# A GRU over 256 steps: the order of loads and of the first products before step 1

## The chip, the core and the metric

The kernel runs on one core of one Trainium2 chip. The metric is the device time of one execution in microseconds (us). The kernel before took 1025.57 us (median of three runs, 1025.18 to 1025.68).

## What is computed

With 16 sequences of 256 steps and 512 channels:

```
x = x + causal_depthwise_conv(x, cond)        # 16 taps per channel, the taps are cond [16, 512]
h = cond                                      # initial state, [16, 512]
for t in range(256):                          # GRU cell, W_ih and W_hh are [512, 1536]
    gi = x[:, t] @ W_ih + b_ih
    gh = h @ W_hh + b_hh
    r = sigmoid(i_r + h_r); z = sigmoid(i_z + h_z)
    n = tanh(i_n + r * h_n)
    h = (1 - z) * n + z * h
    out[:, t] = x[:, t] + h
```

Everything is float32.

## The kernel before, in words

The 512 channels are laid out as four chunks `c` of 128 partitions. The 1536 gate columns are split into two halves `f`, which run a little apart so that one half's gate arithmetic lies beside the other half's matmuls. A **group** is four matmuls of 32 output partitions (j = 0 to 3), which run beside each other in the array, and each of which the trace keeps as two records; so eight records of L328 or L318 are one group.

*Products* (`product(q)`, L318) are x @ W_ih. One q is one group: two steps (index m), a half f and a chunk c. They are done ahead of use: a pair of steps has 8 groups, and 4 groups stand beside every step. *Recurrences* (`recur(t, f, c)`, L328) are h @ W_hh, 8 groups a step. Both add into the PSUM tile `pg[m % 3][f]`, into which ScalarE has copied the biases (`seed`, L437). Within a PSUM tile the h_n part has its own columns (0 to 64), r and z follow, and i_n is last. For a recurrence to write n, r and z as one matmul, ScalarE copies W_hh's n columns in front of its r and z columns (L455). Only for the last chunk of step 0 this copy isn't waited for: `recur_first` makes two matmuls of each (L339 r and z, L342 n).

After a half's last recurrence VectorE turns the gates out of PSUM (L539, L543), ScalarE takes the sigmoids (L461, L463), VectorE forms i_n + r * h_n (L551), ScalarE the tanh (L466), GpSimd z * h (L290) and VectorE h (L564). TensorE's next step waits for that h, and fills the time with products.

Each engine runs its own instructions in the order in which the code writes them; a wait holds everything behind it on that engine. There is no planner. The prologue, up to step 1, in order on each queue:

- SyncE: issues cond, x of the first 16 steps (`xs`), four parts of W_ih (768 KB each), four of W_hh (768 KB each, one semaphore each), then x of later steps.
- ScalarE: issues the two biases, then `scratch` (the padded taps, written to DRAM for later), then makes 16 diagonal matrices of cond (L446), seeds six PSUM tiles (L437), moves the convolution of chunk 3 out of PSUM (L451), loads the sigmoid table and copies W_hh's n columns part by part (L455).
- VectorE: clears two tiles, copies cond to h, lays out the biases (L577 to L585), then convolves chunks 0 to 2 of the first 16 steps (`first`, `rest`), with the two `transpose_in` of i_n (L534) put in before the last LATE = 22 of `rest`.
- TensorE: clears six PSUM tiles (L370), runs WARM = 6 matmuls of zeros (L372), convolves chunk 3 by 17 matmuls (L364), makes 16 product groups (steps 0 to 3), then step 0's recurrences chunk by chunk as W_hh arrives, with 5 and 3 matmuls of zeros (IDLE, L400) behind chunks 0 and 1, then four product groups (`products(0)`), and then step 1.

## Time and profile before

| | us |
|---|---|
| median of three runs | 1025.57 |
| lowest, highest | 1025.18, 1025.68 |
| the profiled execution | 1025.25 |
| its span, first to last instruction | 1023.5 |
| TensorE matmul busy | 1015.4 (99%) |
| VectorE busy | 865.1 (85%) |
| ScalarE busy | 399.3 (39%) |
| GpSimd busy | 237.4 (23%) |

The span lies 1.75 us below the time of the same execution; that rest is start and end outside the instructions. The rows further down show mean durations in ns and starts in us from the start of the span. A merged row of the timeline (x16) gives the start of the first and the time from there to the end of the last of its instructions. A row of PEld is a weight load, of PE the matmul that uses it, of SPq and ACTq a transfer issued by SyncE's or ScalarE's queue.

### The profile page before, as it was taken

To read this page: it belongs to the slowest core of one execution; us is meant where nothing else is said; L and a number is where in the kernel's file an instruction comes from. 1 tells how busy PE (TensorE), PEld (TensorE's weight loads), DVE (VectorE), ACT (ScalarE), POOL (GpSimd) and SP (SyncE) were. 2 spreads that over 40 slices of the span, in tenths; PEclk is the share of its full clock that TensorE was granted. 3 is DMA by queue.
4 is the path that set the end of the run, shared out by engine and by line. 5 is a ranking of instruction groups with operands and counts; after the bars stand their busy time and mean duration, and the time that the engine had idled before them with its cause. 6 is when DMAs were issued, how large, how long until landed. Compare 5 with 4: busy or idle time off the path is not lost.

```text
span 1023.5 us, 58209 instructions
## 1 busy us (share of the span) xinstructions
PE 1015.4 (99%) x24837; PEld 902.6 (88%) x24838; DVE 865.1 (85%) x2851; ACT 399.3 (39%) x1816; POOL 237.4 (23%) x784
## 2 busy tenths in 40 slices
PE   8999999999999999999999999999999999999997
PEld 6988888888888888899999999999999999999986
DVE  7788888888888888888888888888888887777555
ACT  5334333333433343333434333343433333343333
POOL 3222222222222222222222222222222222222222
PEclk9999999999999999999999999999999999999999
DMA  8721001010100101001010010101001000000000
GB/s 297 73 34 39 19 21 30 15 36 19 29 25 12 34 19 34 23 12 35 15 39 19 15 36 11 39 19 29 22 14 35 14 29 16 11 29 4 24 14 12
DMA packets 66450, 32.07 MB, mean 31 GB/s; under 512 B 43920, under 2 KB 65040, under 8 KB 66192
## 3 DMA queue, kind: packets, MB, share of 16 engines
q1 hardware_dynamic: 65760, 28.25, 10.7%
q8 instruction: 195, 3.19, 1.3%
q14 instruction: 63, 0.52, 0.2%
q10 hardware_dynamic: 432, 0.11, 0.0%
HBM read 19.86 MB, written 8.49 MB: 28 GB/s over the span
## 4 chain that ended last, share of the span: by engine, by line
PE 97%; issue 1%; POOL 1%; DVE 0%; DMA 0%; ACT 0%; POOLq 0%; DVEq 0%
PE pg L328 65%; PE pg L318 32%; POOL tz L277 1%; PE pcv L356 0%; DMA cnd<-cond 0%; DVE hp L564 0%; POOL nzh L290 0%; DVE gt L539 0%; DVE gn L543 0%; ACT rz L461 0%; POOL cpad L267 0%; POOL nzh L274 0%; POOL rz L272 0%; POOL zcp L273 0%; POOL cpad L269 0%
## 5 line engine op out<-in xcount | busy, mean ns | idle before, releaser
L328 PE MATMUL pg<-whh,hp 128*32 128x192 f32 x16368 | 716.8, 326 | 2.1 <-ACT whh L455 1.1
L328 PEld LDWEIGHTS pg<-whh,hp 128*32 128x32 f32 x16368 | 594.3, 110 | 74.8 <-DVE hp L564 2.7
L318 PE MATMUL pg<-wih,x 128*32 128x192 f32 x8192 | 385.4, 326 | 0.0
L290 POOL TENSOR_TENSOR nzh<-rz,hp 128x32 f32<-128x32 f32 x512 | 158.0, 309 | 780.0 <-ACT rz L461 780.0
L318 PEld LDWEIGHTS pg<-wih,x 128*32 128x32 f32 x8192 | 296.5, 110 | 35.0
L461 ACT ACTIVATE rz<-gt 128x64 f32<-128x64 f32 x512 | 136.1, 266 | 484.6 <-DVE gt L539 459.1
L506 DVE SCALAR_TENSOR_TENSOR x<-xb,cnd,x 128x512 f32<-128x512 f32 (+1 forms) x420 | 294.6, 702 | 8.0
L564 DVE TENSOR_TENSOR_SCAN hp<-zcp,nzh 128x96 f32<-128x96 f32 x512 | 173.0, 338 | 41.4 <-ACT nzh L466 40.7
L539 DVE STREAM_TRANSPOSE gt<-pg 128x128 f32<-128x128 f32 x512 | 160.2, 313 | 50.8 <-PE pg L328 42.6
L551 DVE TENSOR_TENSOR_SCAN an<-rz,gn 128x64 f32<-128x64 f32 x512 | 148.7, 290 | 52.2 <-ACT rz L461 52.0
L466 ACT ACTIVATE nzh<-an 128x32 f32<-128x32 f32 x512 | 120.8, 236 | 125.6 <-DVE an L551 125.6
L463 ACT ACTIVATE zcp<-gt 128x32 f32<-128x32 f32 x512 | 111.0, 217 | 0.0
L543 DVE STREAM_TRANSPOSE gn<-pg 128x64 f32<-128x64 f32 x512 | 106.5, 208 | 0.0
L437 ACT ACTIVATE pg<-bc 128x256 f32<-128x256 f32 x256 | 86.4, 370 | 0.0
L284 POOL TENSOR_TENSOR x<-x,hp 128x64 f32<-128x64 f32 x255 | 81.5, 320 | 0.0
L534 DVE STREAM_TRANSPOSE gn<-pg 128x64 f32<-128x64 f32 x256 | 57.7, 226 | 0.1
L506 DVE SCALAR_TENSOR_TENSOR x<-xb,cnd 128x512 f32<-128x512 f32 (+1 forms) x28 | 19.3, 688 | 0.0
L490 DVE SCALAR_TENSOR_TENSOR x<-xs,cnd,x 128x192 f32<-128x192 f32 (+11 forms) x45 | 11.6, 335 | 0.0
L517 DVE SCALAR_TENSOR_TENSOR x<-xb,cnd,x 128x512 f32<-128x512 f32 x15 | 10.9, 727 | 0.2
L277 POOL MEMSET tz<- 128x2048 f32 x3 | 5.3, 1805 | 1.0 <-DVE bc L585 1.0
L455 ACT ACTIVATE whh<-whh 128x512 f32<-128x512 f32 x4 | 2.5, 630 | 7.1 <-DMA whh<-w_hh 7.1
L356 PEld LDWEIGHTS pcv<-tz,xw 128*32 128x32 f32 x192 | 5.0, 110 | 0.3
(47 smaller groups left out, 49.4 us busy)
## 6 DMA issues: line engine op xcount, KB each, us to landing
xb<-x SPq DMA_DIRECT2D x96, 94.0 KB, 2.0
out<-x SPq DMA_DIRECT2D x60, 128.0 KB, 1.9
wih<-w_ih SPq DMA_DIRECT2D x4, 768.0 KB, 8.0
whh<-w_hh SPq DMA_DIRECT2D x4, 768.0 KB, 14.2
xw<-x SPq DMA_DIRECT2D x24, 64.0 KB, 3.3
xb<-x SPq DMA_DIRECT2D x16, 62.0 KB, 1.8
tz<-taps SPq DMA_DIRECT2D x12, 64.0 KB, 3.5
xs<-x SPq DMA_DIRECT2D x1, 512.0 KB, 4.6
```

The costliest lines, as they stand in the source:

```text
L290: pool.tensor_tensor(nzh[:, f, ::2, :, 1], chunks(rz[:, f, 1, :, 1]), h_of(t - 1, slice(f * CH, (f + 1) * CH)), ALU.mult).then_inc(s_zh[f], 1)
L318: i = pe.matmul(pg[m % Q][f][D * j:D * (j + 1), RZ:END], x1_of(c, 2 * m, 2 * m + 2), wih[:, c, :, :].rearrange("p (g k) (j d) -> p j g k d ...
L328: i = pe.matmul(pg[t // 2 % Q][f][D * j:D * (j + 1), 0:IN], hp[:, t % 2, 2 * c + 1 - t % 2:2 * c + 3 - t % 2, :, 1].rearrange("p u b -> p ...
L437: act.activation(pg[m % Q][f][:, 0:END], bc[:, f, :], ACT.Copy).then_inc(s_seed[f], 1)
L461: act.activation(rz[:, f, :, :, 1].rearrange("p g (c b) -> p (g c) b", b=B), gt[:, f, :, u], ACT.Sigmoid).then_inc(s_rz[f], 1)
L463: act.activation(zcp[:, f, ::2, :, 1], gt[:, f, CH:, u], ACT.Sigmoid, scale=-1.0).then_inc(s_zc[f], 1)
L466: act.activation(nzh[:, f, ::2, :, 0], chunks(an[:, f, :, 1]), ACT.Tanh).then_inc(s_n[f], 1)
L506: dve.scalar_tensor_tensor(o, xx[:, c, (K - 1 - lag) * B:(K - 1 - lag + n) * B], cnd[:, c, K - 1 - lag:K - lag], o if lag else now, ALU.mu ...
L539: dve.transpose(gt[:, f, :, :].rearrange("p c r -> p (c r)"), pg[t // 2 % Q][f][:, RZ:IN]).then_inc(s_trz[f], 1)
L543: dve.transpose(gn[:, t // 2 % 2, :, f, :, :, 0].rearrange("p u c b -> p c u b"), pg[t // 2 % Q][f][:, 0:RZ]).then_inc(s_tn[f], 1)
L551: dve.tensor_tensor_scan(an[:, f].rearrange("p n s -> p (n s)"), rz[:, f, 0].rearrange("p n s -> p (n s)"), gn[:, t // 2 % 2, t % 2, f].re ...
L564: dve.tensor_tensor_scan(hp[:, (t + 1) % 2, a:a + n].rearrange("p c b s -> p (c b s)"), zcp[:, f, 0:n].rearrange("p c b s -> p (c b s)"), ...
```

## The change

SyncE issues x first and then the weights; cond is issued by ScalarE behind the two biases. The last part of W_hh is loaded as two transfers, r and z (512 KB, `s_whh[3]`), then n (256 KB, `s_whl`), and `recur_first` becomes `recur_rz` and `recur_n`. Of the products of steps 4 and 5, five groups are made in the prologue, where it was four: one behind each of the first three chunks of step 0's recurrence, and two behind the last chunk; step 1 has three in place of four. For these steps chunk 3 is taken first. WARM goes, IDLE for chunk 0 is 3 in place of 5, and LATE is 18 in place of 22. VectorE lays out the biases ahead of copying cond to h, GpSimd clears four tiles ahead of padding the taps, ScalarE issues `scratch` behind the fourth diagonal, and loads the sigmoid table first, on zeros.

The diff:

```diff
--- before.py
+++ after.py
@@ -29,9 +29,8 @@
 NT = TB // QT
 TAPS = 3 * K
 FEW = 4
-WARM = 6
-LATE = 22
-IDLE = {0: 5, 1: 3}
+LATE = 18
+IDLE = {0: 3, 1: 3}
 M2 = T // 2
 RZ, IN, END = CH * D, 3 * CH * D, 4 * CH * D
 Q = 3
...
@@ -154,7 +154,7 @@
             def until(t):
                 n = C * (t + 1) if t <= THIN else C * (THIN + 1) + (C - 1) * (t - THIN)
                 return 2 * H * C + min(n, H * C * (M2 - 2))
-            return range(until(t - 1), until(t))
+            return range(until(t - 1) + (t == 1), until(t))
 
         def inputs(t):
 
@@ -221,12 +221,13 @@
                 sp.wait_ge(s_o, b)
                 sp.dma_start(out[:, c, a * B:b * B], x1_of(c, a, b)).then_inc(s_out[k], 16)
 
-            sp.dma_start(cnd[:, :, :], cond).then_inc(s_cnd, 16)
             sp.dma_start(xs[:, :, :], x[:, :, 0:TB * B]).then_inc(s_xs, 16)
             for c in range(C):
                 sp.dma_start(wih[:, c, :, :], w_ih[:, c, :, :]).then_inc(s_wih[c], 16)
-            for c in range(C):
+            for c in range(C - 1):
                 sp.dma_start(whh[:, c, F:], w_hh[:, c, :]).then_inc(s_whh[c], 16)
+            sp.dma_start(whh[:, C - 1, F:3 * F], w_hh[:, C - 1, 0:2 * F]).then_inc(s_whh[C - 1], 16)
+            sp.dma_start(whh[:, C - 1, 3 * F:], w_hh[:, C - 1, 2 * F:]).then_inc(s_whl, 16)
             sp.wait_ge(s_whh[C - 2], 16)
             sp.dma_start(xb[1][:, 0, :], x[:, 0, B:(W2 + TB) * B]).then_inc(s_xe, 16)
             for t in range(T):
...
@@ -301,12 +302,15 @@
             def product(q):
 
                 m, f, c = q // (H * C), q // C % H, q % C
+                if m == 2:
+                    c = (c - 1) % C
                 if m < 2 and f == 0:
                     pe.wait_ge(s_wih[c], 16)
                 if m < 2 and c < C - 1:
                     pe.wait_ge(s_first, len(FIRST))
+                if q % C == 0:
+                    pe.wait_ge(s_seed[f], m + 1)
                 if c == 0:
-                    pe.wait_ge(s_seed[f], m + 1)
                     if FEW <= 2 * m < TB:
                         pe.wait_ge(s_first, len(FIRST) + len(REST))
                     elif TB <= 2 * m < LONG[0][0]:
@@ -319,7 +323,7 @@
                                   wih[:, c, :, :].rearrange("p (g k) (j d) -> p j g k d", g=3, j=J)
                                   [:, j, :, f * CH:(f + 1) * CH],
                                   start=False, stop=True, skip_group_check=True)
-                if c == C - 1:
+                if q % C == C - 1:
                     i.then_inc(s_gi[f], 1)
 
             def recur(t, f, c):
@@ -331,15 +335,20 @@
                                   start=False, stop=True, skip_group_check=True)
                 return i
 
-            def recur_first(f, c):
-
-                hh = hp[:, 0, 2 * c + 1:2 * c + 3, :, 1].rearrange("p u b -> p (u b)")
+            def recur_rz(f, c):
+
                 for j in range(J):
-                    o = pg[0][f][D * j:D * (j + 1), :]
-                    pe.matmul(o[:, RZ:IN], hh,
-                              whh[:, c, F:3 * F].rearrange("p (g j f n) -> p j f g n", g=2, j=J, f=H)[:, j, f],
-                              start=False, stop=True, skip_group_check=True)
-                    i = pe.matmul(o[:, 0:RZ], hh,
+                    i = pe.matmul(pg[0][f][D * j:D * (j + 1), RZ:IN],
+                                  hp[:, 0, 2 * c + 1:2 * c + 3, :, 1].rearrange("p u b -> p (u b)"),
+                                  whh[:, c, F:3 * F].rearrange("p (g j f n) -> p j f g n", g=2, j=J, f=H)[:, j, f],
+                                  start=False, stop=True, skip_group_check=True)
+                return i
+
+            def recur_n(f, c):
+
+                for j in range(J):
+                    i = pe.matmul(pg[0][f][D * j:D * (j + 1), 0:RZ],
+                                  hp[:, 0, 2 * c + 1:2 * c + 3, :, 1].rearrange("p u b -> p (u b)"),
                                   whh[:, c, 3 * F:].rearrange("p (j f n) -> p j f n", j=J, f=H)[:, j, f],
                                   start=False, stop=True, skip_group_check=True)
                 return i
@@ -368,8 +377,6 @@
             for q in range(Q):
                 for f in range(H):
                     pe.matmul(pg[q][f][:, :], zeros[:, 0:P], zeros[:, :], start=True, stop=True).then_inc(s_bits, 1)
-            for _ in range(WARM):
-                pe.matmul(pcv[0][:, :], zeros[:, 0:P], zeros[:, :], start=True, stop=True)
             pe.wait_ge(s_xs, 16)
             pe.wait_ge(s_eye, 2)
             tap(0, eye[:, :], True)
@@ -387,19 +394,24 @@
             pe.wait_ge(s_tin[1], 1)
             for f in range(H):
                 pe.wait_ge(s_h[f], 1)
-            for c in range(C):
+            for c in range(C - 1):
                 pe.wait_ge(s_whh[c], 16)
-                if c < C - 1:
-                    pe.wait_ge(s_whn, c + 1)
+                pe.wait_ge(s_whn, c + 1)
                 for f in range(H):
-                    if c < C - 1:
-                        recur(0, f, c)
-                    else:
-                        recur_first(f, c).then_inc(s_gh[f], 1)
+                    recur(0, f, c)
+                if c < H:
+                    product((2 * H + c) * C)
                 for _ in range(IDLE.get(c, 0)):
                     pe.matmul(pcv[0][:, :], zeros[:, 0:P], zeros[:, :], start=True, stop=True)
-            for q in products(0):
-                product(q)
+            product(2 * H * C + 1)
+            pe.wait_ge(s_whh[C - 1], 16)
+            for f in range(H):
+                recur_rz(f, C - 1)
+            pe.wait_ge(s_whl, 16)
+            for f in range(H):
+                recur_n(f, C - 1).then_inc(s_gh[f], 1)
+            for c in range(1, C - 1):
+                product(2 * H * C + c + 1)
             pe.wait_ge(s_whn, C)
             for t in range(1, T):
                 m = t // 2
@@ -438,20 +450,23 @@
 
             act.dma_start(bih[:, :], b_ih).then_inc(s_small, 16)
             act.dma_start(bhh[:, :], b_hh).then_inc(s_small, 16)
-            act.wait_ge(s_cp, 3)
-            act.dma_start(scratch[:, :, :], cpad[:, :, :]).then_inc(s_scr, 16)
+            act.dma_start(cnd[:, :, :], cond).then_inc(s_cnd, 16)
+            act.wait_ge(s_clear, 1)
+            act.activation(pre[:, :], zeros[:, 0:B], ACT.Sigmoid)
             act.wait_ge(s_eye, 2)
             act.wait_ge(s_cnd, 16)
             for lag in range(K):
+                if lag == J:
+                    act.wait_ge(s_cp, 3)
+                    act.dma_start(scratch[:, :, :], cpad[:, :, :]).then_inc(s_scr, 16)
                 act.activation(diagonal(lag), eye[:, :], ACT.Copy, scale=cnd[:, C - 1, K - 1 - lag:K - lag]).then_inc(s_dg, 1)
             for m in range(Q):
                 for f in range(H):
                     seed(m, f)
             act.wait_ge(s_c3, 1)
             act.activation(x1[:, C - 1, 0:TB * B], pcv[0][:, 0:TB * B], ACT.Copy).then_inc(s_ev, 1)
-            act.activation(pre[:, :], cnd[:, 0, :], ACT.Sigmoid)
             for c in range(C):
-                act.wait_ge(s_whh[c], 16)
+                act.wait_ge(s_whh[c] if c < C - 1 else s_whl, 16)
                 act.activation(whh[:, c, 0:F], whh[:, c, 3 * F:], ACT.Copy).then_inc(s_whn, 1)
             act.wait_ge(s_zero, 4)
             for t in range(T):
...
```

SyncE's queue from its start; a part of W_hh is `whh<-w_hh`, and the last number is the elements a partition. Before:

```order
L224 DMA cnd<-cond 128x64
L225 DMA xs<-x 128x4x256
L227 DMA wih<-w_ih 128x1536 x4
L229 DMA whh<-w_hh 128x1536 x4
L231 DMA xb<-x 128x752 [waits s_whh2]
```

Now:

```order
L224 DMA xs<-x 128x4x256
L226 DMA wih<-w_ih 128x1536 x4
L228 DMA whh<-w_hh 128x1536 x3
L229 DMA whh<-w_hh 128x1024
L230 DMA whh<-w_hh 128x512
L232 DMA xb<-x 128x752 [waits s_whh2]
```

cond has left the head of the queue, and the last part of W_hh is two transfers.

TensorE from the products of steps 0 to 3 on (L328, L339, L342 of before are L332, L341, L350 of now, L318 is L322, L400 is L405; each x4 is a group). Before, up to the first pair of the last chunk's sixteen matmuls, which alternate in this way:

```order
L318 MATMUL pg<-wih,x 32x192 x64
L328 MATMUL pg<-whh,hp 32x192 x8
L400 MATMUL pcv<-zeros 128x512 x5
L328 MATMUL pg<-whh,hp 32x192 x8
L400 MATMUL pcv<-zeros 128x512 x3
L328 MATMUL pg<-whh,hp 32x192 x8
L339 MATMUL pg<-whh,hp 32x128
L342 MATMUL pg<-whh,hp 32x64
```

Now, up to the products of step 1:

```order
L322 MATMUL pg<-wih,x 32x192 x4
L405 MATMUL pcv<-zeros 128x512 x3
L332 MATMUL pg<-whh,hp 32x192 x8
L322 MATMUL pg<-wih,x 32x192 x4
L405 MATMUL pcv<-zeros 128x512 x3
L332 MATMUL pg<-whh,hp 32x192 x8
L322 MATMUL pg<-wih,x 32x192 x4
L341 MATMUL pg<-whh,hp 32x128 x8
L350 MATMUL pg<-whh,hp 32x64 x8
L322 MATMUL pg<-wih,x 32x192 x8
L332 MATMUL pg<-whh,hp 32x192 x32
L322 MATMUL pg<-wih,x 32x192 x12
```

Product groups stand between the chunks, the last chunk's r and z come for both halves before its n, and two product groups (x8) are left before step 1 and three (x12) in it, where before both places held four (x16).

VectorE, where the turning of i_n (L534, now L549) stands among the convolution (L490, now L505). Before:

```order
L490 SCALAR_TENSOR_TENSOR x<-xs,cnd,x 128x128 x2
L534 STREAM_TRANSPOSE gn<-pg 128x2x2x16 x2
L490 SCALAR_TENSOR_TENSOR x<-xs,cnd,x 128x128
L490 SCALAR_TENSOR_TENSOR x<-xs,cnd,x 128x112 x3
L490 SCALAR_TENSOR_TENSOR x<-xs,cnd,x 128x96 x3
```

Now:

```order
L505 SCALAR_TENSOR_TENSOR x<-xs,cnd,x 128x128 x3
L505 SCALAR_TENSOR_TENSOR x<-xs,cnd,x 128x112 x3
L549 STREAM_TRANSPOSE gn<-pg 128x2x2x16 x2
L505 SCALAR_TENSOR_TENSOR x<-xs,cnd,x 128x96 x3
```

Four operations of the convolution have moved ahead of it.

## Rows read from the trace of the kernel before

**Rows 1.** The page: span, busy time, chain by engine and line

```profile
span 1023.5 us, 58209 instructions
...
PE 1015.4 (99%) x24837; PEld 902.6 (88%) x24838; DVE 865.1 (85%) x2851; ACT 399.3 (39%) x1816; POOL 237.4 (23%) x784
...
PE pg L328 65%; PE pg L318 32%; POOL tz L277 1%; PE pcv L356 0%; DMA cnd<-cond 0%; DVE hp L564 0%; POOL nzh L290 0%; DVE gt L539 0%; DVE gn L543 0%; ACT rz L461 0%; POOL cpad L267 0%; POOL nzh L274 0%; POOL rz L272 0%; POOL zcp L273 0%; POOL cpad L269 0%
```

**Rows 2.** The page, costliest groups: busy us, mean ns of one, idle before, its releaser

```profile
L328 PE MATMUL pg<-whh,hp 128*32 128x192 f32 x16368 | 716.8, 326 | 2.1 <-ACT whh L455 1.1
```

**Rows 3.** Stretches of the start: busy us per engine (instructions), granted clock, DMA share, GB/s

```profile
0.00:5.00 5.00, 3.75 (x9) 1.34 (x10) 2.68 (x10) 1.34 (x2) 2.27 (x13) 1.00 0.52 135
...
15.00:20.00 5.00, 4.04 (x77) 2.42 (x69) 5.00 (x25) 1.26 (x2) 0.00 (x0) 1.00 1.02 417
```

**Rows 4.** Timeline, loads of W_hh and what follows: start us, us, instruction, idle before

```profile
16.06 0.37 DVE L534 STREAM_TRANSPOSE gn<-pg 128x64 f32<-128x64 f32 x2
16.36 4.42 DVE L490 SCALAR_TENSOR_TENSOR x<-xs,cnd,x 128x128 f32<-128x128 f32 x22
...
16.53 0.86 PE L328 MATMUL pg<-whh,hp 128*32 128x192 f32 x16
...
21.25 1.07 PE L328 MATMUL pg<-whh,hp 128*32 128x192 f32 x16 [0.27 <-ACT whh L455]
22.33 0.63 ACT L455 ACTIVATE whh<-whh 128x512 f32<-128x512 f32 x1 [1.22 <-DMA whh<-w_hh]
...
22.98 0.11 PEld L318 LDWEIGHTS pg<-wih,x 128*32 128x32 f32 x1
...
23.01 0.32 DVE L539 STREAM_TRANSPOSE gt<-pg 128x128 f32<-128x128 f32 x1 [2.23 <-PE pg L342]
```

**Rows 5.** Timeline, end of step 0 and start of steps 1 and 2

```profile
24.30 0.36 DVE L564 TENSOR_TENSOR_SCAN hp<-zcp,nzh 128x96 f32<-128x96 f32 x1
...
24.81 2.81 PE L328 MATMUL pg<-whh,hp 128*32 128x192 f32 x64 [0.24 <-DVE hp L564]
...
28.05 0.31 DVE L564 TENSOR_TENSOR_SCAN hp<-zcp,nzh 128x96 f32<-128x96 f32 x1
...
28.70 2.81 PE L328 MATMUL pg<-whh,hp 128*32 128x192 f32 x64
```

**Rows 6.** Timeline, first issues and what they start

```profile
0.81 0.39 SPq L224 DMA_DIRECT2D cnd<-cond  x1
...
1.25 0.45 ACTq L440 DMA_DIRECT2D bhh<-b_hh  x1
...
1.25 0.68 SPq L225 DMA_DIRECT2D xs<-x  x1
...
4.94 4.79 ACT L446 ACTIVATE xb<-eye,cnd 128x128 f32<-128x128 f32 x16
...
5.87 0.68 DVE L480 SCALAR_TENSOR_TENSOR x<-xs,cnd 128x64 f32<-128x64 f32 x3 [0.88 <-DMA xs<-x]
```

**Rows 7.** DMA issues: line, KB each, median us to landing

```profile
taps<-cpad ACTq DMA_DIRECT2D x1, 96.0 KB, 7.3
...
cnd<-cond SPq DMA_DIRECT2D x1, 32.0 KB, 1.8
```

**Rows 8.** Timeline of TensorE before the products

```profile
1.25 2.74 PE L370 MATMUL pg<-zeros 128*128 128x512 bf16 x6 [1.25 <-DVE zeros L569]
...
3.79 2.67 PE L372 MATMUL pcv<-zeros 128*128 128x512 bf16 x6
...
6.73 4.56 PE L364 MATMUL pcv<-xs,xb 128*128 128x256 f32 x32
...
11.22 5.41 PE L318 MATMUL pg<-wih,x 128*32 128x192 f32 x128
```

**Rows 9.** By shape, before 26 us: busy us, mean ns

```profile
L372 PE MATMUL pcv<-zeros 128*128 128x512 bf16 x6 | 2.7, 618 | 0.0
...
L400 PE MATMUL pcv<-zeros 128*128 128x512 bf16 x7 | 1.8, 381 | 0.2 <-issue 0.2
```

More of the change, by code:

```diff
@@ L91, in build @@
         s_whh = [sem(f"s_whh{c}") for c in range(C)]
+        s_whl = sem("s_whl")
         s_whn = sem("s_whn")
@@ L264, in _ @@
                                channel_multiplier=1).then_inc(s_eye, 1)
+            pool.memset(an[:, :, :, :], 0.0).then_inc(s_zero, 1)
+            pool.memset(rz[:, :, :, :, :], 0.0).then_inc(s_zero, 1)
+            pool.memset(zcp[:, :, :, :, :], 0.0).then_inc(s_zero, 1)
+            pool.memset(nzh[:, :, :, :, :], 0.0).then_inc(s_zero, 1)
             pool.wait_ge(s_cnd, 16)
@@ L270, in _ @@
                                ALU.add).then_inc(s_cp, 1)
-            pool.memset(an[:, :, :, :], 0.0).then_inc(s_zero, 1)
-            pool.memset(rz[:, :, :, :, :], 0.0).then_inc(s_zero, 1)
-            pool.memset(zcp[:, :, :, :, :], 0.0).then_inc(s_zero, 1)
-            pool.memset(nzh[:, :, :, :, :], 0.0).then_inc(s_zero, 1)
             pool.wait_ge(s_bc, H)
@@ L570, in _ @@
             dve.memset(hp[:, :, :, :, :], 0.0).then_inc(s_clear, 1)
-            dve.wait_ge(s_cnd, 16)
-            dve.wait_ge(s_clear, 2)
-            for f in range(H):
-                dve.tensor_copy(h_of(-1, slice(f * CH, (f + 1) * CH)),
-                                cnd[:, f * CH:(f + 1) * CH, :]).then_inc(s_h[f], 1)
             dve.wait_ge(s_small, 32)
@@ L587, in _ @@
                               ).then_inc(s_bc, 1)
+            dve.wait_ge(s_cnd, 16)
+            dve.wait_ge(s_clear, 2)
+            for f in range(H):
+                dve.tensor_copy(h_of(-1, slice(f * CH, (f + 1) * CH)),
+                                cnd[:, f * CH:(f + 1) * CH, :]).then_inc(s_h[f], 1)
             dve.wait_ge(s_xs, 16)
```

## The prediction, made before the changed kernel was run

> **What bounds the kernel now.** I read the page's head first: TensorE is busy 99% of a span of 1023.5 us, and its two lines of products and recurrences make up 97% of the chain that ended last [rows 1]. Then the costliest group: 16,368 records of the recurrence, with only 2.1 us of idle time ahead of all of them [rows 2]. So the steps run back to back, and the timeline says at what pace: step 1 starts at 24.81 us and step 2 at 28.70 [rows 5], which is 3.89 us for 12 groups (8 of the recurrence, 4 of products), 0.325 us a group. The change leaves the number of groups as it is. From step 2 on nothing can be gained or lost unless the order there changes, and it doesn't. What is left to look at is the first 25 us.
>
> There the stretches show the DMA engines full from 15 to 20 us (share 1.02) while TensorE has only 4.04 of 5 us [rows 3]: the weights arrive too late. The timeline agrees: chunk 2 of step 0's recurrence starts at 21.25, released by ScalarE's copy, and behind the last part of W_hh (landed by 22.33, where ScalarE's copy of it starts) the last chunk is computed and VectorE turns the first half's gates at 23.01 [rows 4]. From there it is a fixed chain of small operations on four engines, 1.65 us up to the end of h at 24.66 (24.30 + 0.36), and step 1 starts 0.15 us later [rows 5]. So the time ahead of step 1 is set by the landing of W_hh, TensorE's work on the last two chunks, and this chain.
>
> **Part 1, weights earlier.** SyncE issues cond at 0.81 and x at 1.25 [rows 6]. Without cond everything on that queue starts 0.44 us earlier, and with full DMA engines [rows 3] it also lands earlier by that. Bounds: nothing (the engines have the same bytes to move) to 0.44. I take 0.44, since the engines are half idle in the first 5 us (share 0.52) and what is gained there is kept. Chunk 2 then starts at 21.25 - 0.44 = 20.81, the last part is in at 22.33 - 0.44 = 21.89, and its r and z (two thirds of the bytes) some 0.6 us sooner, at 21.3.
>
> **Part 2, TensorE up to the last chunk.** Chunk 2 is 2 groups, 0.65 us, to 21.46. Then comes the product group put in there, 0.325, to 21.79; by then r and z lie ready and n almost. So here the change turns a wait for DMA into work, and TensorE is late by itself. r and z of both halves are 128 of 192 columns, 2 x 0.217 = 0.43, to 22.22. For n, of 64 columns, there are two bounds: a third of a group, 0.11, or what 16 records of mixed 128 and 64 columns took before, (22.98 - 22.35)/31 = 0.020 us a record or 0.16 for eight (the last part's first matmul follows its landing by 0.02, 22.33 to 22.35; by 22.98 31 of its 32 weight loads have started [rows 4]). I take 0.16: the first half ends at 22.38. Before it ended at 22.35 + 0.325 = 22.67. Gain 0.29 us, which the chain passes on whole: VectorE turns gates at 22.72, h is there at 24.37, step 1 starts at 24.52. The second half ends at 22.55 (before: 23.00), and VectorE turned it at 23.92 only, behind the first half's work, so it waits for nothing new. The split itself costs SyncE one more issue, long before use, and no more bytes. If n landed later than 22.22, it would cost one to one; its margin is 0.33.
>
> **Part 3, four or three product groups.** Behind the last chunk now stand two product groups (22.55 to 23.20), so TensorE idles about 1.3 us until 24.52, where it was some 0.5. That idle time costs nothing by itself. The fifth group, gone from step 1, is worth 0.325 if h is early enough. In step 1 h is ready at 28.05 + 0.31 = 28.36, the next step could start 0.15 later, at 28.51, and started at 28.70 [rows 5]. So of the 0.325 us only 0.19 can be had; then VectorE's chain is what the step waits for. Bounds 0.19 and 0.325, I take 0.19.
>
> **Part 4, what could now come late.** (a) The turning of i_n, for which the first chunk waits: it stood at 16.06 and TensorE began at 16.53 [rows 4]. Now x lands 0.44 earlier (VectorE's convolution starts at 5.43, not 5.87 [rows 6]), but four more operations stand ahead: the largest of the 22 that took 4.42 us [rows 4], so above 0.20 each, and below the 0.27 that the 38 ahead of them, with larger ones among them, took on average (5.87 to 16.06), so 0.8 to 1.1; I take 1.0. The first chunk begins at 16.53 - 0.44 + 1.0 = 17.1. From there TensorE has per chunk 0.65 + 0.325 + 3 matmuls of zeros (0.21 each, 0.64) = 1.62 us, so it comes to chunk 2 at 17.1 + 3.24 = 20.34, before 20.81. Margin 0.47. (b) The products of steps 0 to 3 (before from 11.22, 5.41 us [rows 8]) and (c) the convolution of chunk 3 ahead of them, 32 records and two more just ahead, 6.3 to 11.2 [rows 8], now start on the landing of x, about 5.5, 0.8 earlier, since WARM doesn't stand ahead any more: 10.4 and 15.7 as ends. Margin to 17.1: 1.4 us. ScalarE's 16 diagonals take 4.79 us and began at 4.94 behind a table load [rows 6]; the load is now done before, and they begin with cond, issued behind two biases at 1.25 + 0.45 = 1.70. (d) cond's landing: it took 1.8 us at the head of an idle queue, and 96 KB on ScalarE's queue took 7.3 beside the weights [rows 7]. So it is there between 3.5 and 9.0; with a third of those bytes and x alone beside it I take 4.0. Up to 5.4 it costs nothing (x is waited for), up to 5.9 the margin of (a) takes it. (e) The scratch transfer, the clears on GpSimd and the bias layout all have microseconds of room: GpSimd waits 13 us for step 0, and the tiles it clears are needed at 16 us.
>
> (f) WARM. The first six 128x512 matmuls follow each other at (3.79 - 1.25)/6 = 0.42 us: 512 columns at 1.2 GHz. WARM's six take 618 ns each, the same shape 381 ns in IDLE [rows 8, 9], though the granted clock reads 1.00 in both stretches [rows 3]; the durations decide. A group streams its 192 columns in 0.325 us, which is four cycles of 2.4 GHz a column; the 16 taps' 2176 columns (256 + 240 + ... + 16) at 1.2 GHz would then take 7.3 us, and took 4.56 [rows 8]. So the clock rose at about 6 us, after TensorE had been busy from 1.25 on. Now it is busy 1.25 to 4.0, idle to 5.5, and busy from there, so I expect it to rise late. Each microsecond at 1.2 GHz behind 5.5 costs half of one. The margins of (c) and (a), 1.4 and 0.47, take 1.9, that is a low clock up to about 9.3 us. I take about 9.5, and 0.1 us as the cost.
>
> The Trainium skill (TensorE: Matmul & The Clock Gate, section Why this matters for your kernels) asks for a benchmark to warm the array up with matmuls first and warns of idle gaps. It speaks against removing WARM. The first durations of this trace agree with its lower level at the start; by that rule the convolution would run slow, as (f) has it.
>
> **Sum.** -0.29 - 0.19 + 0.1 = -0.38 us. On the profiled execution, 1025.25 us (1023.5 us of span and 1.75 around it), this gives 1024.87. The median shown lies 0.32 above that execution, so as a median I predict 1025.57 - 0.38 = 1025.2 us.
>
> **The rivals.** *Low clock past 9.3 us* (the side of slower). Every further microsecond costs 0.5, and the matmuls of zeros, now on the path, cost twice. At 12.2 us it would be 1.45 more than nothing: 22.38 + 1.45 puts the first half's end at 23.8, 1.2 behind before, less 0.19: 1.0 slower, 1026.5. For it speaks that TensorE is idle for 1.5 us just when it wasn't before; against it only the margins of 1.9 us. *cond lands late*: it decides from 5.9 us. At 7.5 everything behind it on VectorE is 1.6 later and the sum becomes +1.1, 1026.7. For it: the 7.3 us of the other ScalarE transfer; against: few bytes, and issued ahead of the weights. *The DMA engines don't start earlier*: W_hh lands as before, part 2 gives -0.29 + 0.44 = +0.15, part 3 stays, sum about 0: 1025.5. *All goes well*: n at 0.11, the fifth group whole, no cost of the clock: -0.34 - 0.325 = -0.67, 1024.9. *The clock falls in the new idle stretch before step 1*: TensorE idles 1.3 us behind stretches that were only 80% busy [rows 3]. Then the next step or so runs at half speed: 3.9 us for a whole one, 2 to 3.9 in all: 1027.5 to 1029. Against it: the stretch from 15 to 20 us had 0.96 us of idle time as well, and kept the level.
>
> **Chances.** The forecast (-0.6 to -0.1): 0.43. Low clock past 9.3: 0.25. cond late: 0.06. No earlier landing: 0.13. All well: 0.08. Fall of the clock: 0.05. The change does something else than it says: none that I see, since it computes the same groups. About 0.2% (2.05 us) is what a measurement can tell from no change, and only the fall of the clock, or cond at its upper bound (+2.6), reach it: slower 0.04. Faster by 2.05 would need more than the 0.88 us of all upper bounds (0.44 + 0.11 + 0.325): 0.01 is for what I haven't seen. Within: 0.95. The range takes the likeliest, both losses of about 1 us and the gain of 0.7, with the spread of single runs (0.5 us): 1024.2 to 1027.0. The likeliest one's own is 1024.9 to 1025.6.
>
> **What would show it.** x's landing (first convolution on VectorE) at 5.4; the last copy of W_hh's n on ScalarE at 21.9; r and z of the last chunk at 21.8 with no wait for DMA ahead; n's eight first records done by 22.4; VectorE's turning of gates at 22.7; step 1 at 24.5 behind a wait for h of more than 1 us; step 2 3.7 us behind step 1 with a wait of about 0.1 for h; all later steps at 3.89. Part 1 is wrong if the copies of W_hh start when they did. Part 4 is wrong if the first chunk begins behind 17.6, and by the convolution's records it will show whether clock or cond did it: matmuls of 256 columns 0.43 us apart say clock, diagonals that start behind 5.9 say cond.

## The result, and the profile after

The changed kernel took 1027.97 us (median of 11 runs, 1027.51 to 1029.05), the one before 1025.54 (11 runs, 1025.18 to 1025.89): slower by 2.43 us, the ratio is 1.0025 with a 95% interval of 1.0017 to 1.0033. The prediction was 1025.2, with a range up to 1027.0. It was wrong in the sign, and the time lies outside the range. The profiled execution took 1027.63 us with a span of 1025.9; before it was 1025.25 and 1023.5 [rows 1], so the two profiles differ by 2.4 us as the medians do.

The page of the changed kernel, its lines for [rows 1] and [rows 2]:

```profile
span 1025.9 us, 58191 instructions
...
PE 1014.5 (99%) x24829; PEld 883.5 (86%) x24830; DVE 864.7 (84%) x2851; ACT 398.5 (39%) x1815; POOL 238.5 (23%) x784
...
PE pg L332 65%; PE pg L322 32%; DMA cnd<-cond 1%; POOL tz L278 1%; PE pcv L365 0%; DVE hp L579 0%; POOL nzh L291 0%; DVE gt L554 0%; ACTq L452 0%; ACTq L451 0%; DVE gn L558 0%; ACT rz L476 0%; POOL cpad L272 0%; POOL cpad L274 0%; POOLq L44 0%
...
L332 PE MATMUL pg<-whh,hp 128*32 128x192 f32 x16368 | 715.9, 326 | 1.9 <-DVE hp L579 1.9
```

The steps are as they were: the same 16,368 records with 1.9 us of idle time before them. In the chain by lines cond has grown (`DMA cnd<-cond` 1%, it was 0% [rows 1]).

The timeline, its lines for [rows 6] to [rows 8]: start in us, duration in us, instruction, idle time before and its releaser:

```profile
0.81 0.69 SPq L224 DMA_DIRECT2D xs<-x  x1
...
1.56 2.27 SPq L226 DMA_DIRECT2D wih<-w_ih  x4
...
1.70 0.54 ACTq L453 DMA_DIRECT2D cnd<-cond  x1
...
5.32 1.22 PE L373 MATMUL pcv<-xs,eye 128*128 128x256 f32 x2 [1.33 <-DMA xs<-x]
...
8.25 0.69 ACT L462 ACTIVATE xb<-eye,cnd 128x128 f32<-128x128 f32 x2 [4.46 <-DMA cnd<-cond]
8.41 0.66 DVE L495 SCALAR_TENSOR_TENSOR x<-xs,cnd 128x64 f32<-128x64 f32 x3
...
8.70 6.21 PE L373 MATMUL pcv<-xs,xb 128*128 128x256 f32 x32 [2.16 <-ACT xb L462]
...
14.84 5.41 PE L322 MATMUL pg<-wih,x 128*32 128x192 f32 x128
```

cond is issued at 1.70, x has landed by 5.32, and cond is first used at 8.2: ScalarE idles 4.46 us for it, and VectorE's convolution, which needs both, starts at 8.41 in place of 5.87 [rows 6]. The convolution of chunk 3 on TensorE starts at 8.70 and takes 6.21 us where it took 4.56 [rows 8].

The same timeline, its lines for [rows 4] and [rows 5]:

```profile
17.37 0.63 ACT L470 ACTIVATE whh<-whh 128x512 f32<-128x512 f32 x1 [1.25 <-DMA whh<-w_hh]
...
19.29 0.63 ACT L470 ACTIVATE whh<-whh 128x512 f32<-128x512 f32 x1 [1.29 <-DMA whh<-w_hh]
19.59 0.37 DVE L549 STREAM_TRANSPOSE gn<-pg 128x64 f32<-128x64 f32 x2
...
20.07 0.86 PE L332 MATMUL pg<-whh,hp 128*32 128x192 f32 x16
...
21.93 0.86 PE L332 MATMUL pg<-whh,hp 128*32 128x192 f32 x16
22.38 0.63 ACT L470 ACTIVATE whh<-whh 128x512 f32<-128x512 f32 x1 [2.46 <-DMA whh<-w_hh]
...
23.80 0.86 PE L332 MATMUL pg<-whh,hp 128*32 128x192 f32 x16
...
25.60 0.32 DVE L554 STREAM_TRANSPOSE gt<-pg 128x128 f32<-128x128 f32 x1 [2.29 <-PE pg L350]
...
27.40 2.81 PE L332 MATMUL pg<-whh,hp 128*32 128x192 f32 x64 [1.10 <-DVE hp L579]
...
31.10 2.81 PE L332 MATMUL pg<-whh,hp 128*32 128x192 f32 x64
```

The first chunk of step 0 starts at 20.07 (16.53 before [rows 4]), right behind VectorE's turning of i_n. Of these 3.54 us 2.54 are the later start of VectorE's convolution, and 1.0 are the four operations that were moved ahead of the turning; by then two more parts of W_hh are there (17.37, 19.29), so the chunks follow each other without a wait for DMA, 1.87 us apart (a **chunk cycle** from here on). Step 1 starts at 27.40 (24.81 before [rows 5], 2.59 later), step 2 at 31.10 (28.70, 2.40 later). The 2.40 us is the whole difference of the spans.

### The profile page after: what moved, and what is told of

The parts are those of the page before. It is cut to its first block, busy times and chain, and to the rows that moved or that the text cites. A ratio compares the mean times of both kernels' runs of the same rounds, so it can differ in the third digit from the quotient of the medians.

```text
span 1025.9 us, 58191 instructions
## 1 busy us (share of the span) xinstructions
PE 1014.5 (99%) x24829; PEld 883.5 (86%) x24830; DVE 864.7 (84%) x2851; ACT 398.5 (39%) x1815; POOL 238.5 (23%) x784
## 3 DMA queue, kind: packets, MB, share of 16 engines
HBM read 19.86 MB, written 8.49 MB: 28 GB/s over the span
## 4 chain that ended last, share of the span: by engine, by line
PE 97%; issue 1%; DMA 1%; POOL 1%; DVE 0%; ACTq 0%; ACT 0%; POOLq 0%; DVEq 0%
PE pg L332 65%; PE pg L322 32%; DMA cnd<-cond 1%; POOL tz L278 1%; PE pcv L365 0%; DVE hp L579 0%; POOL nzh L291 0%; DVE gt L554 0%; ACTq L452 0%; ACTq L451 0%; DVE gn L558 0%; ACT rz L476 0%; POOL cpad L272 0%; POOL cpad L274 0%; POOLq L44 0%
## 5 line engine op out<-in xcount | busy, mean ns | idle before, releaser
L332 PE MATMUL pg<-whh,hp 128*32 128x192 f32 x16368 | 715.9, 326 | 1.9 <-DVE hp L579 1.9
L332 PEld LDWEIGHTS pg<-whh,hp 128*32 128x32 f32 x16368 | 581.1, 110 | 87.4 <-issue 3.6
L322 PE MATMUL pg<-wih,x 128*32 128x192 f32 x8192 | 385.2, 326 | 0.0
L322 PEld LDWEIGHTS pg<-wih,x 128*32 128x32 f32 x8192 | 290.5, 110 | 40.9
L549 DVE STREAM_TRANSPOSE gn<-pg 128x64 f32<-128x64 f32 x256 | 57.5, 225 | 0.1
L505 DVE SCALAR_TENSOR_TENSOR x<-xs,cnd,x 128x192 f32<-128x192 f32 (+11 forms) x45 | 11.6, 332 | 0.0
L373 PEld LDWEIGHTS pcv<-xs,xb 128*128 128x128 f32 x32 | 5.7, 230 | 3.3 <-ACT xb L462 2.9
L373 PE MATMUL pcv<-xs,xb 128*128 128x256 f32 (+15 forms) x32 | 6.2, 362 | 2.2 <-ACT xb L462 2.2
L462 ACT ACTIVATE xb<-eye,cnd 128x128 f32<-128x128 f32 x16 | 4.8, 389 | 4.5 <-DMA cnd<-cond 4.5
```

The source lines that it names most:

```text
L322: i = pe.matmul(pg[m % Q][f][D * j:D * (j + 1), RZ:END], x1_of(c, 2 * m, 2 * m + 2), wih[:, c, :, :].rearrange("p (g k) (j d) -> p j g k d ...
L332: i = pe.matmul(pg[t // 2 % Q][f][D * j:D * (j + 1), 0:IN], hp[:, t % 2, 2 * c + 1 - t % 2:2 * c + 3 - t % 2, :, 1].rearrange("p u b -> p ...
```

## The experiments

All medians are of 11 runs (5 in the third and fourth), beside 21 to 33 runs of the kernel before with medians of 1025.55 to 1025.61. The intervals of the ratios are about 0.1% wide on either side, so what lies between 1024.6 and 1026.6 can't be told from no change by them; there the text goes by the medians and by the times inside the profiles, and a profile is one execution. One of the 33 runs of the kernel before beside experiments 5 to 8 took 2186.47 us; it moves neither the median nor the ratios. Theory C: cond's late landing is the loss. Rival W: TensorE's clock, which rises late without WARM, is.

**1. cond first again.**

```diff
+            sp.dma_start(cnd[:, :, :], cond).then_inc(s_cnd, 16)
             sp.dma_start(xs[:, :, :], x[:, :, 0:TB * B]).then_inc(s_xs, 16)
-            act.dma_start(cnd[:, :, :], cond).then_inc(s_cnd, 16)
```

> The changed kernel with cond issued first on SyncE's queue again, ahead of x. Theory C (cond's late landing costs the time): cond lands at about 2.6 us, VectorE's convolution starts with x at 5.9, the first chunk at about 17.5, and the whole comes to 1025.1 to 1025.7. Rival W (TensorE's clock rises late because WARM is gone, whatever cond does): the convolution of chunk 3 and part of the products still run at 1.2 GHz up to 9 to 12 us, and the whole stays at 1026.3 or above.

Measured: 1025.63 us (1025.29 to 1026.82). Its timeline:

```profile
6.01 0.68 DVE L495 SCALAR_TENSOR_TENSOR x<-xs,cnd 128x64 f32<-128x64 f32 x3 [1.67 <-DMA xs<-x]
...
7.04 6.16 PE L374 MATMUL pcv<-xs,xb 128*128 128x256 f32 x32
...
17.70 0.51 DVE L549 STREAM_TRANSPOSE gn<-pg 128x64 f32<-128x64 f32 x2 [0.42 <-PE pg L323]
...
18.35 0.83 PE L333 MATMUL pg<-whh,hp 128*32 128x192 f32 x16
...
25.66 2.81 PE L333 MATMUL pg<-whh,hp 128*32 128x192 f32 x64 [1.10 <-DVE hp L579]
```

In the medians all of the loss is back (1025.63 beside 1025.61 of the kernel before), with the convolution on TensorE still slow (6.16 us). So the slow convolution alone is not the loss, and W falls. The clock now shows as the second term: VectorE waits 0.42 us for the products that the slow convolution has delayed.

**2. WARM back, cond late.**

```diff
+            for _ in range(6):
+                pe.matmul(pcv[0][:, :], zeros[:, 0:P], zeros[:, :], start=True, stop=True)
             pe.wait_ge(s_xs, 16)
```

> The changed kernel with the six WARM matmuls back; cond stays third on ScalarE's queue. Theory C: cond still lands at about 8.2 us and VectorE turns i_n at 19.6, so the time stays at 1027.5 to 1027.7, only the runs above 1028.5 go, since those would be the ones with a late clock. Rival W: the clock is up by 8.7 us, and the whole falls to 1026.3 or below.

Measured: 1027.72 us (1027.58 to 1028.59), 0.25 below the changed kernel. Where the changed kernel had four of eleven runs above 1028.6, the highest is now 1028.59. WARM brings back almost nothing while cond is late, as theory C has it. Alone this run wouldn't rule out the clock, since the clock isn't up when the convolution runs; it takes experiment 1 for that. Stretches of this run: length, TensorE busy us (records), granted clock, DMA share, GB/s:

```profile
5.00:9.00 4.00, 1.54 (x6) 0.94 1.02 395
9.00:12.00 3.00, 3.00 (x8) 0.52 1.01 422
12.00:15.00 3.00, 3.00 (x26) 1.00 1.03 387
```

It had risen: the two matmuls ahead of the convolution, which start at 5.84, took 0.70 us, against 1.22 in the changed kernel. TensorE then waited for cond (busy 1.54 of 4 us, idle from 6.54 on), the granted clock was 1.00 from 8.00 to 8.25 and 0.50 from 8.50 to 9.00, and it stayed at the lower level (0.52) just as the convolution ran, which again took 6.08 us.

**3. cond first on ScalarE, the biases behind it.**

```diff
+            act.dma_start(cnd[:, :, :], cond).then_inc(s_cnd, 16)
             act.dma_start(bih[:, :], b_ih).then_inc(s_small, 16)
             act.dma_start(bhh[:, :], b_hh).then_inc(s_small, 16)
-            act.dma_start(cnd[:, :, :], cond).then_inc(s_cnd, 16)
```

> The changed kernel with cond issued by ScalarE ahead of the two biases, beside x on SyncE's queue. If cond was late because it stood third behind the biases, it lands before x (5.3 us) and the time is 1025.1 to 1025.7. If it was late because x and the weights on the other queue take the DMA engines meanwhile, it still lands after 6 us, and the time stays above 1026.5, though the biases are late instead and may hold the seeds.

Measured: 1029.08 us (1028.80 to 1030.56), worse than the change. Its DMA issues, KB and us from issue to landing, and under them those of the changed kernel:

```profile
taps<-cpad ACTq DMA_DIRECT2D x1, 96.0 KB, 6.9
...
cnd<-cond ACTq DMA_DIRECT2D x1, 32.0 KB, 1.9
bih<-b_ih ACTq DMA_DIRECT2D x1, 6.0 KB, 4.4
bhh<-b_hh ACTq DMA_DIRECT2D x1, 6.0 KB, 6.7
```

```profile
taps<-cpad ACTq DMA_DIRECT2D x1, 96.0 KB, 6.8
...
cnd<-cond ACTq DMA_DIRECT2D x1, 32.0 KB, 6.5
bih<-b_ih ACTq DMA_DIRECT2D x1, 6.0 KB, 1.7
bhh<-b_hh ACTq DMA_DIRECT2D x1, 6.0 KB, 3.7
```

The first transfer of ScalarE's queue lands in 1.7 to 1.9 us, the second in 3.7 to 4.4, the third in 6.5 to 6.7, whether it is 32 KB of cond or 6 KB of a bias. So between 6 and 32 KB the size doesn't matter. Whether it is the place in the queue that counts, or the time of the issue, these three can't say, since both change together (they are issued at 0.81, 1.2 and 1.7 us, and W_ih from 1.56 on). The scratch transfer (`taps<-cpad`) speaks for the time: issued here at 3.58, while both biases were still under way (they landed at 5.6 and 8.4), it took 6.9 us, and in the changed kernel, issued at 8.81 with everything ahead of it landed, 6.8. What stands ahead in ScalarE's queue did not change it; beside it SyncE's queue was streaming in both. No run separates the two for cond itself.

Here cond was early, but the bias, whose layout stands ahead of the convolution in VectorE's order, landed at 8.4, and the convolution began at 9.64. Of my expectation the first half had the landing right, and the second the time and the late biases.

**4. The issue order alone, on the kernel before.**

```diff
-            sp.dma_start(cnd[:, :, :], cond).then_inc(s_cnd, 16)
...
             act.dma_start(bhh[:, :], b_hh).then_inc(s_small, 16)
+            act.dma_start(cnd[:, :, :], cond).then_inc(s_cnd, 16)
```

> The kernel before with one part of the change alone: x is first on SyncE's queue and cond third on ScalarE's. Theory C: cond lands at about 8 us; behind it stand VectorE's bias layout, the padding of the taps, ScalarE's scratch transfer and its table load, so this costs more than the whole change did, about 2.5 to 3.5 us: 1028 to 1029. Rival W: WARM is there, so the order alone costs under 0.8 us: below 1026.4.

Measured: 1030.87 us (1029.43 to 1031.03). The order of issue alone costs 5.3 us, more than expected. In the old order the bias layout, the table load and the diagonals all stand behind cond. The clock has a part in it too: in the profiled run, at 1029.43 the fastest of the five, TensorE idled from 7.36 to 11.09 us and the granted clock was 0.50 from 11 to 14; over the whole run it was 0.998 there and 0.996 in the four slower ones. All the other parts of the change together win back some 3 us (1030.87 against 1027.97) of what its first part loses; which of them do, no run shows.

**5. cond first and WARM: both causes undone.** Experiment 1 with the lines of experiment 2.

> The changed kernel with cond first on SyncE's queue and the six WARM matmuls back. In the run with cond first alone the convolution of chunk 3 took 6.16 us in place of 4.56, its products ended at 18.5 us, VectorE waited 0.42 us for them, and step 1 began at 25.66. Theory C with a second term for the clock: with WARM the products end by 16.8, VectorE turns i_n at 17.3, the first chunk begins at 17.7, chunk 2 at 21.5, step 1 at 25.1: 1025.2 to 1025.4 and narrower. Rival I (the work put between the chunks is what remains): chunk cycles stay at 1.87 us either way. If WARM doesn't matter at all: 1025.6 as without it.

Measured: 1025.27 us (1025.08 to 1026.35), 0.36 below experiment 1. In the profile the convolution takes 4.56 us again, the first chunk starts at 17.53, step 1 at 25.00. WARM is worth some 0.4 us here in the medians. Chunks 1 and 2 start at 19.52 and 21.43, 1.99 and 1.91 us apart, each 0.15 behind the end of ScalarE's copy (which starts at 18.74 and 20.65 and takes 0.63), so here the landing of W_hh and TensorE's cycle of 1.87 us are level.

**6. No zeros between the chunks, cond late.**

```diff
-IDLE = {0: 3, 1: 3}
+IDLE = {}
```

> The changed kernel, cond still late, without the 3 + 3 matmuls of zeros behind chunks 0 and 1. Theory I: because the first chunk starts at 20.1 us, every part of W_hh is there and TensorE is the bound: its cycle of 1.87 us a chunk (0.65 recurrence, 0.33 products, 0.6 matmuls of zeros, 0.3 to 0.4 gaps around them) falls to 0.98, twice: 1.7 us less, 1026.2 to 1026.4. Rival (the late chain on VectorE or the last landing at 22.4 us sets the end): under 0.5 us less.

Measured: 1027.46 us (1026.60 to 1027.98). Most of it missed: 0.5 us less in the median, and 0.9 between the fastest runs (1026.60 and 1027.51). Its timeline shows two reasons; the profiled execution is the slowest of the eleven (1027.98), so they needn't hold for the others:

```profile
8.67 7.70 PE L373 MATMUL pcv<-xs,xb 128*128 128x256 f32 x32 [2.79 <-ACT xb L462]
...
20.87 0.50 DVE L549 STREAM_TRANSPOSE gn<-pg 128x64 f32<-128x64 f32 x2 [1.24 <-PE pg L322]
...
21.53 0.83 PE L332 MATMUL pg<-whh,hp 128*32 128x192 f32 x16
...
22.50 0.83 PE L332 MATMUL pg<-whh,hp 128*32 128x192 f32 x16
...
24.78 0.53 PE L322 MATMUL pg<-wih,x 128*32 128x192 f32 x8 [0.47 <-DVE x L505]
```

The cycle did fall to 0.97 us. But the first chunk started 1.46 later, behind a convolution slowed further by the clock (7.70 us, with a granted clock of 0.50 from 9 to 14 us), and the product group behind chunk 2, the first to need chunk 0 of x's convolution, waited 0.47 us for VectorE to end it. Behind TensorE's cycle lay a second limit that I hadn't priced.

**7. The split and the product groups alone, all else as before.** WARM 6, LATE 22, and the order of every other engine as before; zeros 3 and 3.

> The kernel before with only the split of W_hh's last part and the five product groups (and 3 matmuls of zeros in place of 5); queues, WARM, LATE and the order on the other engines as before. cond lands at 2.6 us. By the prediction's part 2 without the earlier landing: chunk 2 at 21.25, the product group to 22.2, r and z to 22.7, the first half's n at 22.85, step 1 at 24.95 to 25.0 in place of 24.81; part 3: step 2 follows 3.71 us behind it in place of 3.89: sum about 0: 1025.4 to 1025.7. If the product group behind chunk 2 costs nothing: 1025.2. If the gaps around the added groups push chunk 2 late as well: 1025.9 and above.

Measured: 1025.34 us (1024.95 to 1026.14). Step 1 starts at 24.86 and step 2 at 28.56, 0.14 ahead of before. So these parts bring 0.1 us in the profile and 0.2 in the medians, which the interval doesn't tell from nothing. The profile has it from step 1, as part 3 of the prediction did: step 1 takes 3.70 us in place of 3.89.

**8. cond behind x on SyncE.**

```diff
             sp.dma_start(xs[:, :, :], x[:, :, 0:TB * B]).then_inc(s_xs, 16)
+            sp.dma_start(cnd[:, :, :], cond).then_inc(s_cnd, 16)
```

with five WARM, LATE 22, IDLE empty, and `product(2 * H * C + 1)` moved behind `recur_rz`.

> A version meant to beat both: the changed kernel with cond issued by SyncE right behind x, five WARM matmuls, LATE 22, no matmuls of zeros between the chunks, and the group behind chunk 2 moved between r and z, and n, of the last chunk. Theory: cond lands in x's train, at 5.5 us, the convolutions start at 5.6 to 6.2, the first chunk begins at 16.9, chunk 2 at 20 to 20.7, and the end hangs on the last landing of W_hh, at 22.3 or before: step 1 at 24.5, and 1025.0 to 1025.3. If cond behind x on the same queue comes as late as on ScalarE's: above 1026.5.

Measured: 1024.83 us (1024.52 to 1026.43), the lowest median of all: 0.7 below the kernel before in the medians, ratio 0.9994 (0.9985 to 1.0003), so not apart from it by the interval, though ten of its 11 runs lie below the lowest one of before.

```profile
5.39 0.70 ACT L464 ACTIVATE xb<-eye,cnd 128x128 f32<-128x128 f32 x2 [2.18 <-DMA cnd<-cond]
...
5.98 0.67 DVE L497 SCALAR_TENSOR_TENSOR x<-xs,cnd 128x64 f32<-128x64 f32 x3
...
16.63 0.86 PE L333 MATMUL pg<-whh,hp 128*32 128x192 f32 x16
...
21.00 0.86 PE L333 MATMUL pg<-whh,hp 128*32 128x192 f32 x16 [0.71 <-ACT whh L472]
...
22.41 0.43 PE L351 MATMUL pg<-whh,hp 128*32 128x64 f32 x16
...
24.59 2.81 PE L333 MATMUL pg<-whh,hp 128*32 128x192 f32 x64 [1.09 <-DVE hp L581]
```

cond, in x's train on the same queue, is used at 5.4.

**9. The group behind n instead.**

```diff
-            product(2 * H * C + 1)
             pe.wait_ge(s_whl, 16)
...
-            for c in range(1, C - 1):
+            for c in range(C - 1):
```

> The best version so far (cond behind x, five WARM, LATE 22, no zeros between chunks) with the product group that stood between r and z, and n, of the last chunk put behind n, so that three groups lie in the idle stretch before step 1. There n started at 22.41 with its data in at 22.12, and TensorE then idled 1.09 us. Theory: n starts at 22.15, step 1 0.26 us earlier (24.33), 1024.5 to 1024.65. Rival (the idle stretch isn't free, the third group pushes step 1, or the end hangs on something else): 1024.8 or more.

Measured: 1025.00 us (1024.46 to 1025.74): the gain isn't there. In this profile W_hh's last part came at 22.51 (22.12 in experiment 8) and n started at 22.53 behind it, step 1 at 24.72. The third group in the idle stretch did no harm (0.78 us idle is left), but the landing sets the end, and it varies between profiles by more than the 0.26 us looked for.

**10. The changed kernel with one line moved.** cond behind x as in experiment 8, nothing else.

> The changed kernel with one line moved: cond issued by SyncE right behind x, no longer by ScalarE. Everything else as changed (no WARM, LATE 18, zeros between the chunks). Theory C: cond lands at 5.3 us in place of 8.2, VectorE turns i_n 2.4 us earlier, and of the 2.4 us lost nearly all comes back: 1025.3 to 1026.0, the spread by the late clock. If the place of cond in ScalarE's queue were only part of it: above 1026.5.

Measured: 1025.30 us (1025.11 to 1025.66). Its timeline:

```profile
5.90 0.67 DVE L495 SCALAR_TENSOR_TENSOR x<-xs,cnd 128x64 f32<-128x64 f32 x3
...
24.88 2.81 PE L333 MATMUL pg<-whh,hp 128*32 128x192 f32 x64 [1.10 <-DVE hp L579]
```

One line gives back 2.67 us of the median. In this profile the convolution on TensorE started at 5.78 and took 4.78 us: the clock rose in time without WARM. TensorE had been idle for 1.11 us before x came; in experiment 12, with 1.26 us, it took 6.65. The slow convolution without WARM isn't there in every execution.

**11. scratch later** (on experiment 9).

```diff
+                if c == C - 1:
+                    act.wait_ge(s_cp, 3)
+                    act.dma_start(scratch[:, :, :], cpad[:, :, :]).then_inc(s_scr, 16)
                 act.wait_ge(s_whh[c] if c < C - 1 else s_whl, 16)
```

> The version with nothing before n, and the scratch transfer (96 KB) issued by ScalarE behind the copy of chunk 2, when W_hh's last part is nearly in, in place of behind the fourth diagonal. Theory (with TensorE out of the way the last landing of W_hh sets step 1, and the DMA engines are full from 4 us on): W_hh lands 0.2 to 0.3 us earlier, 0.2 us less than the version it is built on. Rival (the straggling engine, not the bytes, sets the last landing, or SyncE's loads behind scratch come late for step 4): no gain, or 0.1 to 0.5 slower.

Measured: 1025.62 us (1024.81 to 1025.83), 0.6 worse than experiment 9. The profiled run took 1024.93, the second fastest of the eleven. Its timeline and its waits:

```profile
21.72 0.43 PE L351 MATMUL pg<-whh,hp 128*32 128x64 f32 x16
...
23.92 2.81 PE L333 MATMUL pg<-whh,hp 128*32 128x192 f32 x64 [0.79 <-DVE hp L580]
```

```profile
PE pg L333 <- DVE hp L580: 0.8, 1, 0.8
PE pcv L366 <- DMA xw<-x: 0.6, 1, 0.6
```

```profile
19.86 3.94 DMA taps<-cpad
...
44.60 3.17 DMA xw<-x
```

W_hh's n was used at 21.72, and step 1 started at 23.92, 0.67 ahead of experiment 8. That the later scratch transfer did it isn't shown, since without it this landing came between 21.1 and 22.7 us. All of it was given back between 44 and 50 us: step 5 still starts 0.66 ahead (44.11 and 44.77), step 6 is 0.14 behind (49.71 and 49.57). In between, near 47 us, TensorE waits 0.56 us for `xw`: SyncE issues its strided loads one behind the other, the first of them waits for scratch, and the chain runs from scratch's landing (issued at 19.86) through some 20 us of issues to that load. It is the move of scratch that put this queue in the way: behind it SyncE's loads begin at 23.87, in experiments 8 and 9 at 20.68 and 21.09, and there TensorE waits for none of them. Why the median is 0.6 worse, the profile of so fast a run doesn't show.

**12. Experiment 8 without WARM.**

> The version with cond behind x and the group before n, without its five WARM matmuls. Clock theory: the convolution of chunk 3 runs 1.6 us longer (6.2 in place of 4.6) or more, products end at 18 to 19.5 in place of 16.5; with no zeros between the chunks TensorE catches up half of it before W_hh's chunk 2 (copy ready at 20.9): 1024.9 to 1025.3 and up to 1026 in single runs. If the clock's margin is as the prediction had it (1.9 us free): no difference, 1024.8.

Measured: 1025.35 us (1025.20 to 1026.52), 0.52 above experiment 8. In the profile the convolution takes 6.65 us, VectorE waits 1.10 us for the products and the first chunk starts at 18.08 in place of 16.63. But by chunk 2 TensorE has caught up: it waits 1.36 us for ScalarE's copy, which starts at 20.48 (20.23 in experiment 8), and begins at 21.57, 0.46 behind the copy's end where it was 0.14. So WARM's 0.5 us is measured in the medians, while this profile doesn't show the path by which it is lost.

## Why the prediction was wrong

**The step that failed is part 4 (d), the landing of cond.** I took 4.0 us, "with a third of those bytes and x alone beside it". It landed at 8.15: 1.70 + 6.45. I had the upper bound of 9.0 from the 7.3 us of the scratch transfer [rows 7] and talked it down by two reasons that were both wrong. The size doesn't matter between 6 and 32 KB (experiment 3), and x wasn't alone beside it: SyncE issued W_ih from 1.56 us on, before cond's own issue. I also had the price of it, 1 to 1 from 5.9 us on, and gave that rival 0.06. The first chunk started at 20.07, not 17.1: 2.97 late, as much as VectorE's convolution (8.41, not 5.43: 2.98). Experiments 1 and 10 undo this alone and get 2.3 and 2.7 us back. In sum step 1 came 2.88 us later than forecast (27.40, not 24.52): 2.97 for the first chunk, less the margin of 0.47 that the forecast had before chunk 2, plus 0.38 because from the first chunk to step 1 it took 7.33 us, where the forecast's terms make 6.95.

**Part 1, weights earlier: right for two parts, not for the last.** Chunks 1 and 2 of W_hh came 1.2 us sooner (17.37 and 19.29 for 18.60 and 20.48), the last part did not: 22.38 for 22.33 [rows 4]. The two of the kernel before:

```profile
18.60 0.63 ACT L455 ACTIVATE whh<-whh 128x512 f32<-128x512 f32 x1 [2.33 <-DMA whh<-w_hh]
...
20.48 0.63 ACT L455 ACTIVATE whh<-whh 128x512 f32<-128x512 f32 x1 [1.25 <-DMA whh<-w_hh]
```

Across the profiles the last part is used between 21.1 (experiments 4 and 6) and 22.7 (experiment 1). In eleven of the fourteen one part takes 2.7 to 3.3 us in place of the 1.9 of the others (3.0 between 15.6 and 18.6 before, 3.1 between 19.3 and 22.4 in the changed kernel). Something the profiles show may bear on it: in each of the fourteen the queue of instructions moves one packet of 0.02 MB between 14.5 and 21.5 us, in the eleven in the late part's stretch or within 0.7 us ahead of it (between 15.5 and 16.5 us before, between 18.5 and 19.5 in the changed kernel). In experiments 4 and 6 it comes latest, after 19.5 and 20.5, and there the last part was used earliest. No run tests whether it is the cause. So the 0.44 us of this part, and with it the 0.29 of part 2, didn't come: in experiment 10, with cond in time, step 1 starts at 24.88, where it started at 24.81 before.

**Part 2: right in its kind.** r and z took 0.44 us (predicted 0.43), and VectorE turned the first half's gates 1.80 us behind chunk 2's start, by the prediction 1.91. In the changed kernel both lay ready by then, so the wait for DMA that it was to fill wasn't there.

**Part 3: right.** Step 2 follows step 1 by 3.70 us (predicted 3.7) with TensorE idle 1.10 us before step 1 and no fall of the clock there: step 1's recurrences take 2.81 us as before [rows 5]. (TensorE's idle time there was 0.24 us before [rows 5], not "some 0.5".)

**Part 4 (a): a term mis-sized.** The cycle of a chunk is 1.87 us, not 1.62. The matmuls of zeros bring some 0.25 us of gaps ("issue" waits of TensorE) around them. The margin before chunk 2 was none: in experiment 10 chunk 2 starts at 21.29, 0.36 us behind the end of ScalarE's copy, where a chunk that waits for the copy starts 0.14 to 0.15 behind it. The 1.0 us for the four operations of the convolution was right.

**Part 4 (f), the clock: the direction right, the margin wrong.** It rose late, and the lack of WARM cost 0.36 us (medians of experiments 1 and 5) and 0.52 (12 and 8), not the 0.1 allowed. Both differences are smaller than their intervals; of the first one the profiles show the path. In the changed kernel, with cond late, putting WARM back brought 0.25 us (experiment 2). The rule of the Trainium skill to warm up with matmuls first (TensorE: Matmul & The Clock Gate, section Why this matters for your kernels) holds here in kind: the convolution took 4.56 us with WARM (experiment 5) and 6.16 without (experiment 1), though 4.78 without it in experiment 10. It isn't enough to warm up, either: in experiment 2 the level fell again in a wait for cond, with a granted clock of 0.52 from 9 to 12 us.

## What to carry to other kernels

Moving a small load off a busy queue onto another one is no way to make it early: ask what streams on the other queue when it is issued, and if it must be early issue it ahead of that stream, or on the same queue right behind the large load that is needed with it. When a bound from a real row (7.3 us) and a story about sizes disagree, the chance belongs to the row. A few microseconds of a prologue are a chain of near-ties: once cond was in time, the clock, the chunk cycle and W_hh's last landing together moved step 1 by about 1 us (24.59 to 25.66 in experiments 1, 5, 8 and 10), so a gain at one is worth only its lead over the next.

## What the runs showed of the hardware

- Transfers on ScalarE's queue with x and W_ih streaming on SyncE's from 0.81 us on landed 1.6 to 1.9, 3.4 to 4.4 and 6.4 to 6.8 us after their issue as first, second and third, with 6 or 32 KB alike in the third place. With x issued only 0.44 us later (the kernel before, experiments 1, 5 and 7) the second landed in 1.7 to 2.1. The 96 KB of scratch, issued between 3.2 and 9.1 us, took 6.6 to 8.4, and 3.9 when issued at 19.86, with W_hh nearly in (experiment 11).
- The same 32 KB of cond issued on SyncE's queue behind 512 KB of x took 3.7 to 3.9 us (experiments 8 to 12), issued on ScalarE's at about the same time 6.4 to 6.8.
- TensorE's clock rose and fell within the prologue: 0.94 from 5 to 9 us, 0.52 from 9 to 12 and 1.00 after (experiment 2). The convolution took 4.6 us at the higher level and 5.8 to 7.7 us with all or part of it at the lower. The granted clock doesn't always show this: it reads 1.00 throughout in the changed kernel, in experiment 1 and in experiment 12, where the convolution took 6.21, 6.16 and 6.65 us.
- Three 128x512 matmuls of zeros between two runs of small ones cost 0.9 us a cycle (1.87 against 0.97), 0.64 of it their own time at the 0.21 us each of the prediction.
